# Down product of the last four units as seven block products

## The reference, cut to what matters

```
x = x + tanh(g_xattn) * attention_mix(layernorm(x), ctx_1024)     # 4 x 512 x 512
wu, wg, wd = ternary(W_up), ternary(W_gate), ternary(W_down)      # sign {-1,0,1} times one scale each
up, gate = layernorm(x) @ wu.T, layernorm(x) @ wg.T               # 4 x 512 x 2048
x = x + tanh(g_ffn) * ((silu(up) * gate) @ wd.T)                  # 4 x 512 x 512
```

## Time and profile before

| | |
|---|---|
| runs of the kernel before | 406.39 us median (405.24 to 406.89, 3 runs) |
| the profiled execution, its own time | 405.63 us |
| its span, first to last instruction | 403.8 us |
| PE busy | 398.3 us (99%) |
| DVE, ACT, POOL busy | 278.8, 254.9, 91.8 us |
| granted TensorE clock | 1.000 of full speed (2.4 GHz) over the whole span |

### The profile page before, as it was taken

How to read it: one execution, slowest core, us unless ns; L and a number is a source line. 1 busy time by engine, 2 the same in 40 slices (tenths; PEclk the granted TensorE clock), 3 DMA queues, 4 the chain that set the end, 5 groups by cost and what they waited for, 6 DMA issues and landing times.

```text
span 403.8 us, 5456 instructions
## 1 busy us (share of the span) xinstructions
PE 398.3 (99%) x1721; PEld 189.8 (47%) x1736; DVE 278.8 (69%) x402; ACT 254.9 (63%) x337; POOL 91.8 (23%) x147
## 2 busy tenths in 40 slices
PE   8999999999999999999999999999999999999997
PEld 6545555454444444444444444444444444444444
DVE  0576578988899984889788875656565747566422
ACT  3886898889767786868888746643426464625300
POOL 0234254658865022314155000000000000000000
PEclk9999999999999999999999999999999999999999
DMA  8999939598600030020019522142300000000023
GB/s 300 412 418 394 387 118 236 132 282 184 157 0 3 0 105 0 10 96 0 1 30 231 110 49 54 52 156 79 131 0 2 0 2 1 0 2 0 2 78 131
DMA packets 42029, 43.88 MB, mean 109 GB/s; under 512 B 30865, under 2 KB 31121, under 8 KB 39953
## 3 DMA queue, kind: packets, MB, share of 16 engines
q1 hardware_dynamic: 42000, 43.53, 34.3%
HBM read 29.89 MB, written 6.29 MB: 90 GB/s over the span
## 4 chain that ended last, share of the span: by engine, by line
PE 83%; DVE 5%; ACT 4%; issue 4%; DMA 2%; SPq 1%; POOL 0%; DVEq 0%; ACTq 0%; POOLq 0%
PE pair L671 27%; PE pair L599 20%; PE pair L601 20%; PE pair L528 8%; PE pair L503 3%; PE pair L489 3%; DMA xf<-in_wdT 2%; PE pair L514 1%; DMA xf<-in_first 1%; DVE x_sb L1064 1%; ACT xf L900 1%; DVE small L1069 1%; SPq L325 1%; PE pair L544 1%; DVE xf L1178 1%
## 5 line engine op out<-in xcount | busy, mean ns | idle before, releaser
L599 PE MATMUL pair<-xb_hi,w_sb 128*128 128x512 f16 x448 | 169.8, 379 | 0.7 <-DVE c L1188 0.3
L601 PE MATMUL pair<-xb_lo,w_sb 128*128 128x512 f16 x448 | 169.8, 379 | 0.0
L671 PE MATMUL pair<-x_sb,sh 128*128 128x512 bf16 (+1 forms) x513 | 110.2, 372 | 0.9
L671 PEld LDWEIGHTS pair<-x_sb,sh 128*128 128x128 f16 x528 | 51.4, 98 | 59.7 <-DVE x_sb L1224 1.0
L599 PEld LDWEIGHTS pair<-xb_hi,w_sb 128*128 128x128 bf16 x448 | 43.8, 98 | 55.5 <-issue 1.6
L900 ACT ACTIVATE xf<-xf,small 128x512 f32<-128x512 f32 x48 | 34.6, 722 | 55.7 <-DVE xf L1183 30.1
L601 PEld LDWEIGHTS pair<-xb_lo,w_sb 128*128 128x128 bf16 x448 | 43.8, 98 | 52.4 <-issue 0.3
L1224 DVE SCALAR_TENSOR_TENSOR x_sb<-pair,small,x_sb 128x512 f32<-128x512 f32 x55 | 41.2, 749 | 28.7 <-PE pair L671 28.4
L528 PE MATMUL pair<-sh,xt_sb 128*128 128x512 f32 (+2 forms) x160 | 57.4, 508 | 0.0
L1188 DVE SCALAR_TENSOR_TENSOR xf<-xf,small 128x512 f32<-128x512 f32 x48 | 37.6, 785 | 13.6 <-ACT xf L900 13.6
L906 ACT ACTIVATE sh<-xf 128x512 f16<-128x512 f32 x48 | 29.7, 626 | 26.0 <-PE pair L671 18.0
(11 more groups left out here) (108 smaller groups left out, 412.2 us busy)
## 6 DMA issues: line engine op xcount, KB each, us to landing
w_sb<-in_wugT SPq DMA_DIRECT2D x8, 1024.0 KB, 10.5
xt_sb<-in_xT SPq DMA_DIRECT2D x16, 256.0 KB, 5.0
x_sb<-in_x SPq DMA_DIRECT2D x4, 1024.0 KB, 9.4
xf<-in_wdT SPq DMA_DIRECT2D x4, 1024.0 KB, 6.3
xt_sb<-in_wdT SPq DMA_DIRECT2D x4, 1024.0 KB, 5.1
out<-x_sb SPq DMA_DIRECT2D x15, 256.0 KB, 2.0
x_dram<-x_sb SPq DMA_DIRECT2D x8, 256.0 KB, 3.4
x_sb<-x_dram SPq DMA_DIRECT2D x2, 1024.0 KB, 5.6
```

Source lines behind the costliest of these rows:

```text
L599: pe.matmul(dst[:, m * 512:(m + 1) * 512], w[:, o:o + P], hi[:, k], start=start and k == 0, stop=False, skip_group_check=not start)
L601: last = pe.matmul(dst[:, m * 512:(m + 1) * 512], w[:, o:o + P], lo[:, k], start=False, stop=k == 1, skip_group_check=not start)
L671: ins = pe.matmul(dst, h_part(n, c, lo)[:, i * P:(i + 1) * P], t_d[:, e * DM + lo_col:e * DM + hi_col], start=first and n == units[0] and ...
```

## The change

The down product of units 12 to 15 is a product of a two by two block matrix of h (rows: even and odd batch; columns: the two hidden halves) with a two by two block matrix of the weights (rows: the two hidden halves; columns: the two halves of 256 output columns). Eight block products become seven, again in Winograd's form.

POOL makes the sums. Once the down weights are ready it makes T1 to T4 of all four units in four operations of 128x1024 in 16 bits (`last_t`, in the place of weights no longer used). In each of units 12 to 15 it makes S3 = h11 - h12, S1 = h12 + h22, S2 = h22 - S3 and S4 = h21 - S2 in f32 (128x512 each), and the low parts of S3 and S4. ACT makes the high parts of S1 to S4 (`high_s`), DVE the low parts of S1 and S2 (`low_s`). The high and low parts of h12 are no longer made in these units. `HS`, the scale of h, goes from 2^-3 to 2^-5.

PE runs `final(j, t)` for the products j = 1 to 7 and the token tiles t = 0 to 3: four units, high and low, eight matmuls of 256 columns each. Products that share a bank are added up there without being cleared (1, then 6, then 7, then 4; and 5, then 3), and DVE adds each prefix sum to its own quarter of the output rows (`final_evict`, 28 evictions of 128x256 in the order `FIN`), so a product waits until the one before it in its bank has been evicted. `copy_1`, `copy_u2`, `copy_5` and `silu` of "21" wait, in these units, also for the POOL sum that reads their buffer. DVE's order for unit 15 is written out. Behind what the diff shows, PE goes on with 3 and 4 for t = 0 and 1, then 5, 2, 6, 3, 7, 4 for t = 2 and 3, each pair after the eviction that it needs. SP stores three tiles of batch 2 and 3 in another order; the last tile goes in two halves of columns as before, but of batch 3.

```diff
-    HS = 2.0 ** -3
+    HS = 2.0 ** -5
...
+        FIN = ([(j, t) for j, first in ((1, 0), (1, 2), (6, 0), (5, 0), (7, 0), (2, 0), (3, 0), (4, 0)) for t in (first, first + 1)] +
+               [(j, t) for j in (5, 2, 6, 3, 7, 4) for t in (2, 3)])
+        OPERAND = {1: "11", 2: "21", 3: "S4", 4: "22", 5: "S1", 6: "S2", 7: "S3"}
+        WEIGHT = {1: (0, 0), 2: (1, 0), 3: (1, 1), 4: "T4", 5: "T1", 6: "T2", 7: "T3"}
+        TARGET = {1: (0, 0), 2: (0, 0), 3: (0, 1), 4: (1, 0), 5: (1, 1), 6: (0, 1), 7: (1, 1)}
...
+        def fin_bank(j, t):
+            return bank[{1: (0, 1, 6, 7), 6: (0, 1, 6, 7), 7: (0, 1, 6, 7), 4: (0, 1, 6, 7),
+                         5: (2, 3, 2, 3), 3: (2, 3, 2, 3), 2: (4, 5, 4, 5)}[j][t]][:, 0:256]
...
+            hold(pool, s_tda, 3)
...
+            pool.tensor_tensor(last_t("T1"), last_td(0, 1), last_td(0, 0), ALU.subtract).then_inc(s_tw, 1)
+            pool.tensor_tensor(last_t("T3"), last_td(1, 1), last_td(0, 1), ALU.subtract).then_inc(s_tw, 1)
+            hold(pool, s_tw, 1)
+            pool.tensor_tensor(last_t("T2"), last_td(1, 1), last_t("T1"), ALU.subtract).then_inc(s_tw, 1)
+            hold(pool, s_tw, 3)
+            pool.tensor_tensor(last_t("T4"), last_td(1, 0), last_t("T2"), ALU.subtract).then_inc(s_tw, 1)
+            def h_of(n, c):
+                return cb(n, c)[:, 0:512]
+            def low_s(n, c):
+                hold(pool, s_shi[c], n - LAST_D + 1)
+                pool.tensor_tensor(sum_part(n, c, 1), sum_f32(c), sum_part(n, c, 0), ALU.subtract).then_inc(s_slo[c], 1)
+            for k in range(4):
+                n = LAST_D + k
+                hold(pool, s_mul["12"], n + 1)
+                if k > 0:
+                    hold(pool, s_slo["S3"], k)
+                pool.tensor_tensor(sum_f32("S3"), h_of(n, "11"), h_of(n, "12"), ALU.subtract).then_inc(s_sh["S3"], 1)
+                hold(pool, s_mul["22"], n + 1)
+                if k > 0:
+                    hold(pool, s_slo["S1"], k)
+                pool.tensor_tensor(sum_f32("S1"), h_of(n, "12"), h_of(n, "22"), ALU.add).then_inc(s_sh["S1"], 1)
+                hold(pool, s_sh["S3"], k + 1)
+                if k > 0:
+                    hold(pool, s_slo["S2"], k)
+                pool.tensor_tensor(sum_f32("S2"), h_of(n, "22"), sum_f32("S3"), ALU.subtract).then_inc(s_sh["S2"], 1)
+                low_s(n, "S3")
+                hold(pool, s_mul["21"], n + 1)
+                hold(pool, s_sh["S2"], k + 1)
+                if k > 0:
+                    hold(pool, s_slo["S4"], k)
+                pool.tensor_tensor(sum_f32("S4"), h_of(n, "21"), sum_f32("S2"), ALU.subtract).then_inc(s_sh["S4"], 1)
+                low_s(n, "S4")
...
+            def final(j, t, units, first, last):
+                for u in units:
+                    c = OPERAND[j]
+                    ready, count = hidden_ready(u, c)
+                    pe.wait_ge(ready, count)
+                    w = WEIGHT[j]
+                    cols = last_t(w)[:, u - LAST_D, :] if j >= 4 else last_td(*w)[:, u - LAST_D, :]
+                    for lo in range(2):
+                        ins = pe.matmul(fin_bank(j, t), hidden(u, c, lo)[:, t * P:(t + 1) * P], cols,
+                                        start=first and u == units[0] and lo == 0,
+                                        stop=last and u == units[-1] and lo == 1, skip_group_check=j in (3, 4, 6, 7))
+                if last:
+                    ins.then_inc(s_fin, 1)
...
             pe.wait_ge(s_mul["21"], n)
             pe.wait_ge(s_ev, 4 * LAST_D)
-            expand(bank[0], ends, 0, 0, True, False)
+            for t in range(2):
+                final(1, t, ends + (n,), True, True)
             product4(n)
-            expand(bank[1], ends, 0, 1, True, False)
+            pe.wait_ge(s_tw, 4)
             pe.wait_ge(s_c["11"], NN)
-            expand(bank[2], ends + (n,), 1, 0, True, True)
-            expand(bank[3], ends + (n,), 1, 1, True, True)
+            for t in range(2):
+                final(5, t, ends, True, False)
+            for t in range(2):
+                pe.wait_ge(s_ef, fin_done(1, t))
+                final(6, t, ends, False, False)
             pe.wait_ge(s_c["12"], NN)
-            expand(bank[4], ends + (n,), 1, 2, True, True)
-            expand(bank[5], ends + (n,), 1, 3, True, True)
-            expand(bank[0], (n,), 0, 0, False, True)
-            expand(bank[1], (n,), 0, 1, False, True)
+            for t in range(2):
+                final(2, t, ends, True, False)
             pe.wait_ge(s_mul["21"], NN)
-            expand(bank[6], ends + (n,), 0, 2, True, True)
-            expand(bank[7][:, 0:DM // 2], ends + (n,), 0, 3, True, True, 0, DM // 2)
-            pe.wait_ge(s_ev, 4 * LAST_D + 1)
-            expand(bank[2][:, 0:DM // 2], ends + (n,), 0, 3, True, True, DM // 2, DM)
+            for t in range(2, 4):
+                final(1, t, ends + (n,), True, True)
+            for t in range(2):
+                final(6, t, (n,), False, True)
+            for t in range(2):
+                final(5, t, (n,), False, True)
+            for t in range(2):
+                pe.wait_ge(s_ef, fin_done(6, t))
+                final(7, t, ends + (n,), False, True)
+            for t in range(2):
+                final(2, t, (n,), False, True)
...
+            def high_s(n, c):
+                act.wait_ge(s_sh[c], n - LAST_D + 1)
+                if c == "S1":
+                    act.wait_ge(s_dt, 4 * d_half_done(n, "12"))
+                act.activation(sum_part(n, c, 0), sum_f32(c), ACT.Copy).then_inc(s_shi[c], 1)
...
+                if n > LAST_D:
+                    high_s(n - 1, "S1")
+                    high_s(n - 1, "S2")
...
+                if n > LAST_D:
+                    high_s(n - 1, "S4")
+                if LAST_D <= n < NN - 1:
+                    high_s(n, "S3")
+                elif 3 <= n < LAST_D:
                     high_h(n, "12")
...
+                if n == NN - 1:
+                    high_s(n, "S3")
                 if n + 1 < NN:
                     copy_1(n + 1)
...
+            high_s(NN - 1, "S1")
+            high_s(NN - 1, "S2")
             high_h(NN - 1, "21")
+            high_s(NN - 1, "S4")
...
+            def low_s(n, c):
+                hold(dve, s_shi[c], n - LAST_D + 1)
+                dve.tensor_tensor(sum_part(n, c, 1), sum_f32(c), sum_part(n, c, 0), ALU.subtract).then_inc(s_slo[c], 1)
...
+            def final_evict(j, t):
+                dve.wait_ge(s_fin, fin_done(j, t))
+                held = {2: 1, 3: 6, 7: 5}.get(j)
+                if held:
+                    hold(dve, s_ef, fin_done(held, t))
+                dve.scalar_tensor_tensor(fin_rows(j, t), fin_bank(j, t), c_out[:, :], fin_rows(j, t),
+                                         ALU.mult, ALU.add).then_inc(s_ef, 1)
...
-            for n in range(NN):
-                down = 3 <= n < NN - 1
+            for n in range(NN - 1):
+                down = 3 <= n
...
+            n = NN - 1
+            make_h(n - 1, "21")
+            make_h(n, "11")
+            add_12(n)
+            low_h(n, "11")
+            add_22(n)
+            make_h(n, "12")
+            low_s(n - 1, "S1")
+            low_s(n - 1, "S2")
+            final_evict(1, 0)
+            make_h(n, "22")
+            final_evict(1, 1)
+            low_h(n - 1, "21")
+            low_h(n, "22")
+            make_h(n, "21")
+            low_s(NN - 1, "S1")
+            low_s(NN - 1, "S2")
+            for j, t in FIN[2:]:
+                final_evict(j, t)
+                if (j, t) == (6, 1):
+                    low_h(NN - 1, "21")
```

More of the change, by code:

```diff
@@ L228, in h_part, with sum_f32, sum_part, hidden @@
             return h_ring[n % 4][:, o:o + 512]
+        def sum_f32(c):
+            return xf[:, 4096 + SUMS.index(c) * 512:4096 + (SUMS.index(c) + 1) * 512]
+        def sum_part(n, c, lo):
+            if c == "S1":
+                return h_part(n, "12", lo)
+            k = ((n - LAST_D) * 3 + SUMS.index(c) - 1) * 2 + lo
+            for home, size in ((xt_flat, 8), (xf[:, 6144:8192], 8), (t3_flat, 4), (early, 4)):
+                if k < size:
+                    return home[:, k * 256:(k + 1) * 256].bitcast(F16)
+                k -= size
+        def hidden(n, c, lo):
+            return h_part(n, c, lo) if c in HSLOT else sum_part(n, c, lo)
+        def hidden_ready(n, c):
+            return (s_lo[c], n + 1) if c in HSLOT else (s_slo[c], n - LAST_D + 1)
+        def last_td(r, c):
+            view = t_d[:, 8 * DM:16 * DM].rearrange("p (u r c n) -> p u r c n", u=4, r=2, c=2)
+            return view[:, :, r, c, :]
+        def last_t(blk):
+            m, u = {"T1": (0, 0), "T2": (0, 4), "T3": (1, 0), "T4": (1, 4)}[blk]
+            units = wbf[:, m, :].rearrange("p (u c) -> p u c", u=NU)
+            return units[:, u:u + 4, A21 * 256:(A21 + 1) * 256]
+        def fin_done(j, t):
+            return FIN.index((j, t)) + 1
+        def fin_bank(j, t):
```

(31 more changed lines are left out.)

43 lines of the change are left out of this document (29 added, 14 removed).

## The result

The changed kernel takes **407.66 us** (median of 12 runs, 406.89 to 408.49), the kernel before 405.77 (12 runs). The ratio is 1.0045, with a 95% interval of 1.0032 to 1.0059: 1.9 us slower, where the forecast was 1.6 slower. The interval lies wholly above 1, so the slowdown is clear of the noise, which is smaller here than the half a per cent that the prediction allowed for. The measured time lies 0.3 us from the 408.0 predicted.

A forecast was written before the change was run, and what follows sets the result against it. The prediction took PE to bound the kernel: -3.4 saved, +0.6 in unit 14 and +4.4 in unit 15 give +1.6 us on 406.39, so 408.0 us; its own range was 406.8 to 409.2, with rivals 403.2 to 410.0.

The forecast's parts named there:

- What PE saves: Last part on PE: 224 matmuls of 256 columns replace 112 of 512 and 32 of 256, saving 3.4 us.
- POOL's price: A POOL f32 operation of 128x512 takes 1.25 us alone and 1.11 behind a DVE operation.
- The bound of 1.44: Upper bound in us for one POOL f32 operation of 128x512, half of the whole 2.88.
- rival 2: Slower case: POOL's f32 operation costs 1.44 us, so the kernel takes 409.4 us; chance 0.2.
- Unit 14: In its `down_half`, PE waits 0.6 us for an eviction behind a delayed `make_h` of "12"; bounds 0 and 1.1.
- The walk through unit 15: Operation-by-operation times for unit 15, with PE waits that sum to 4.4 us and none after 386.
- Weight sums at nothing: POOL's four weight sums in unit 8 or 9 cost PE nothing; without cover, up to 0.5 us.
- The last store: At the kernel's end, SP's 256 KB store of (3,2) starts 0.9 us before the last; cost 0 to 0.3.
- The sum: Whole kernel: -3.4 + 0.6 + 4.4 = +1.6 us, on the median of 406.39, giving 408.0 us.
- Rival 1: Faster case: POOL's f32 operations don't exclude DVE's or miss them, so the kernel takes 403.4 us; chance 0.25.
- ACT is late by less each time: Unit 15: ACT's delays are smaller than DVE's; `silu` of "21" is done at 379.15 and has slack.

The follow-up runs named there:

- e1: Changed kernel with POOL's six operations in each of units 12 to 15 replaced by pairs of memsets that read nothing, so sums are zero; 403.23 us.
- e2: Changed kernel with POOL's six operations in each of units 12 to 15 working on one column of the 512; 403.45 us.
- e7: Changed kernel with unit 15's sums on DVE, POOL's low parts moved, several beside DVE's PSUM reads, and ACT's high parts reordered by need; 404.69 us.
- e10: e7 with the low part of "21"(14) earlier on DVE, S3(15) in its place, ACT's high part of S3 behind `silu` of "21"; 403.99 us.
- e11: e10 with the low part of S1(15) moved from DVE to POOL; 403.62 us.
- e5: Changed kernel with unit 15's six POOL operations moved to DVE, laid into its order by need; POOL keeps units 12 to 14; 405.88 us.

## Why the prediction was right

By its own steps:
- **What PE saves.** Predicted 3.4, measured 3.2: 32 starts of 256 columns span 3.49 us (391.37 to 394.86), 0.109 each and not 0.108, times 192. The earlier trace rows had it: 5.1 less 8 x 0.216 over 31 steps is 0.1087, which the prediction rounded down.
- **POOL's price.** Taken as 1.25 alone; the f32 sums take 1.27, and the low parts with a 16-bit output 1.16. The bound of 1.44 is out, and rival 2 with it.
- **Unit 14.** Predicted 0.6, measured 0.48, for the reason given: `make_h` of "12" ends 0.55 after POOL's low part of S4(13), the eviction comes behind it, and the last tile of the `down_half` behind that.

```profile
354.74 1.46 POOL L551 TENSOR_TENSOR xf<-xf 128x512 f16<-128x512 f32 x1 [2.87 <-ACT xf L1056]
355.10 1.65 DVE L1356 SCALAR_TENSOR_TENSOR xf<-xf,small 128x512 f32<-128x512 f32 x1
356.66 0.74 DVE L1396 SCALAR_TENSOR_TENSOR x_sb<-pair,small,x_sb 128x512 f32<-128x512 f32 x1
357.46 1.90 PE L764 MATMUL pair<-x_sb,sh 128*128 128x512 bf16 x8 [0.32 <-DVE x_sb L1396]
```

- **The walk through unit 15.** In the order of the walk (product 4, (6,0), (6,1), product 2, product 1, product 6, product 7), predicted 0.1, 0.8, 0.4, 0.4, 1.5, 0.9, 0.3; measured 0.1, 0.78, 0.40, 0.53, 1.46, 0.83, 0.31. Sum 4.4 and 4.4. No wait follows after 388, as predicted.
- **Weight sums at nothing.** So it was: the lead of 0.9 us of the profiled execution before is the same ahead of them and behind them, and PE has 8.95 of 9.00.
- **The last store.** Predicted 0 to 0.3, measured 0.2.
- **The sum.** -3.2 + 0.5 + 4.4 + 0.2 = 1.9, measured 1.9. The forecast had 1.6 because the saving was 0.2 too large and the store was left at 0, with 0.1 too much for unit 14 against it. As a time it stood on the median of three runs, 406.39; twelve runs give 405.77, and on them the same sum says 407.4, 0.3 below the measured time and not 0.3 above it. The base was a matter of luck; the terms of the +1.6 hold one by one.
- **Rival 1** (POOL's operations beside DVE's, 403.4) is what e1 and e2 show once POOL reads nothing or next to nothing: 403.23 and 403.45. As a forecast of the changed kernel it fell, since the exclusion was there in f32 too.
- **A step that was wrong.** "ACT is late by less each time: `silu` "21" is done at 379.15 and has slack." It started at 381.37; less the 0.9 of the loading phase and the 0.48 of unit 14, that is 380.0, so it was done at 380.7, 1.5 later than in the walk. The walk had left out its wait for the low part of "21"(14). In the changed kernel this costs nothing, since DVE was busy with the low part of "22" until then. In e7 it cost 0.9, and the expectation of that run was wrong for it.

What stays open: whether e10 or e11 is the faster one, what the place of the low part of "22" is worth in e5, and the cause of the 0.9 us of the loading phase, which differs between executions (the add of "12" in unit 12 starts between 312.57 and 314.55 over all these kernels).

## What to carry to other kernels

A helper engine isn't free because it is idle: ask which operations of its neighbour it shuts out, and whether the bounding engine waits for one of those. In this kernel's last unit an operation of 0.6 us on the busy engine was cheaper than one of 1.2 us on the idle one that stopped the busy one for up to 1.1. Lay the helper's reads beside work that doesn't compete, here DVE's operations that read PSUM, and off the chain that the bounding engine waits for a held-up operation is free. And when fewer matmuls are bought with a longer chain of small operations, walk the last stage of that chain operation by operation, with every wait of every buffer: the columns saved (3.2 us) were smaller than the waits of one unit (4.4 us), and putting the same operations in another place and order gave 3.7 us back.

## What the runs showed of the hardware

From 374 to 387 us of the changed kernel DVE and POOL alternate one operation each wherever both have one with two SBUF inputs, also in f32: a blocked low part (0.68 alone) ends 0.55 us after POOL's operation, and a blocked POOL operation 1.12 (f32 output) or 1.02 (16-bit output) after DVE's. POOL's memsets of 128x512 take 0.53 us in f32 as in 16 bits, and beside them DVE's operations keep their 683 and 747 ns (e1).
